# Silu and the last steps of the group statistics move from VectorE to Pool

## What is computed

```
x = x + L0(gn(x))     # a lattice of 4 x 4 convolution cells with relu
x = x + L1(gn(x))     # a convolution with circular padding
x = x + L2(gn(x))     # spline convolution: silu(p) * base + sum of 8 cubic splines(p) * weights, + bias
x = x + L3(gn(x))     # a plain 3 x 3 convolution, + bias
gn(v) = (v - mean) / sqrt(var + 1e-5)
```

## Time and profile before

| | |
|---|---|
| median of 3 runs | 1281.83 us (1278.43 to 1287.19) |
| the profiled execution | 1273.52 us, of which 1271.7 span |
| busy share of the span | PE 93%, PEld 70%, DVE 60%, ACT 53%, POOL 29% |
| chain that ended last | PE 62%, SPq 15%, DVE 10%, issue 5%, DMA 4%, ACT 3% |
| granted TensorE clock, mean | 0.976 |

### The profile page before, as it was taken

The page is one execution under the profiler, slowest core; times in us unless marked ns, Lnnn a source line. Parts: engine busy times, 40 slices in busy tenths (PEclk is TensorE's granted clock), DMA queues, the critical chain, the costliest instruction groups (busy, mean ns, idle before and its releaser), DMA issues.

```text
span 1271.7 us, 15020 instructions
## 1 busy us (share of the span) xinstructions
PE 1188.8 (93%) x5174; PEld 884.7 (70%) x5174; DVE 768.2 (60%) x975; ACT 674.6 (53%) x736; POOL 370.6 (29%) x544
## 2 busy tenths in 40 slices
PE   2799999999999999989999999999999987999995
PEld 2666677666666677766666677777777766777773
DVE  6799952475575522256565552236665689999962
ACT  1578853454444434354544443444445598789821
POOL 6212333434501022312222314534144331103212
PEclk9899999999999999999999999999999888999997
DMA  6899998999999768899999988879898214676774
GB/s 149 237 253 277 281 271 237 199 177 202 200 195 233 207 178 219 198 196 215 207 181 192 223 202 217 248 203 229 194 202 167 44 30 71 107 113 107 123 122 62
DMA packets 104687, 234.22 MB, mean 184 GB/s; under 512 B 36884, under 2 KB 49764, under 8 KB 96164
## 3 DMA queue, kind: packets, MB, share of 16 engines
q1 hardware_dynamic: 82624, 181.90, 65.5%
q0 software_dynamic: 15808, 24.31, 10.3%
q10 hardware_dynamic: 6180, 27.06, 6.8%
HBM read 124.15 MB, written 85.75 MB: 165 GB/s over the span
## 4 chain that ended last, share of the span: by engine, by line
PE 62%; SPq 15%; DVE 10%; issue 5%; DMA 4%; ACT 3%; POOL 0%; DVEq 0%; ACTq 0%; POOLq 0%
PE PB L1731 53%; SPq L807 12%; PE PB L1700 7%; DVE S L1560 2%; DVE S L1566 2%; DMA F<-F 1%; SPq L786 1%; DMA lattice<-S 1%; DVE S L1573 1%; DVE F L1553 1%; PE PB L1691 1%; SPq L838 1%; ACT F L1142 1%; DVE F L1453 1%; DMA S<-lattice 1%
## 5 line engine op out<-in xcount | busy, mean ns | idle before, releaser
L1731 PE MATMUL PB<-F,WA 128*96 128x512 f32 (+1 forms) x3792 | 916.8, 403 | 23.3 <-DVE F L1465 11.1
L1731 PEld LDWEIGHTS PB<-F,WA 128*96 128x96 f32 (+1 forms) x3792 | 662.7, 176 | 268.5 <-issue 19.8
L1153 ACT ACTIVATE S<-PB,BIAS 96x512 f32<-96x512 f32 (+1 forms) x320 | 212.2, 683 | 304.0 <-PE PB L1731 299.6
L1142 ACT ACTIVATE F<-S 128x2116 fp32r<-128x2116 f32 (+4 forms) x160 | 261.4, 1634 | 188.5 <-DMA lattice<-S 67.3
L1453 DVE TENSOR_TENSOR F<-S,F 128x1089 fp32r<-128x1089 f32 (+2 forms) x80 | 121.4, 1518 | 175.1 <-ACT F L1142 174.1
L1455 DVE TENSOR_TENSOR F<-S,F 128x1058 fp32r<-128x1058 f32 x64 | 80.8, 1263 | 185.5 <-ACT F L1142 185.0
L1465 DVE CAST F<-F 64x528 fp32r<-64x528 f32 (+4 forms) x304 | 183.7, 654 | 3.5
L1700 PE MATMUL PB<-F,WA 128*128 128x512 f32 x576 | 147.4, 414 | 15.1 <-DVE F L1553 15.1
L905 POOL DMA_DIRECT2D WA<-taps x76 | 54.1, 714 | 359.4 <-ACT S L1153 317.5
L1700 PEld LDWEIGHTS PB<-F,WA 128*128 128x128 f32 x576 | 112.5, 197 | 44.3 <-issue 15.8
L1456 DVE TENSOR_TENSOR F<-S,F 64x1058 fp32r<-64x1058 f32 x64 | 79.8, 1247 | 0.0
(11 more groups left out here) (130 smaller groups left out, 745.5 us busy)
## 6 DMA issues: line engine op xcount, KB each, us to landing
S<-lattice SPq DMA_DIRECT2D x448, 66.1 KB, 5.2
lattice<-S SPq DMA_DIRECT2D x32, 817.5 KB, 6.7
S<-lattice SPq DMA_DIRECT2D x160, 136.1 KB, 3.4
S<-lattice SPq DMA_DIRECT2D x72, 272.5 KB, 5.1
lattice<-S SPq DMA_DIRECT2D x52, 272.5 KB, 4.0
lattice<-S ACTq DMA_DIRECT2D x48, 272.5 KB, 4.6
lattice<-S ACTq DMA_DIRECT2D x16, 817.5 KB, 6.6
S<-lattice SPq DMA_DIRECT2D x160, 70.1 KB, 3.4
```

The source lines that it names most:

```text
L1142: act.activation(piece_view(s, h, 0), raw_view(s, h), ACT.Copy).then_inc(hi_ready, 1)
L1153: act.activation(wide(to[:, at:at + TS])[:, :, 0:RX], pixels(RING_BANK[n % SLOTS_O][0:cell.rows, :]), ACT.Relu, bias=BIAS[0:cell.rows, k:k ...
L1731: last = nc.tensor.matmul(bank, WA[0:rows, first:first + cell.rows], wide(FZ[0:rows, i % SLOTS_F, base:base + TS])[:, :, 0:RX], start=j == ...
```

## The change

Four things change. Pool computes silu instead of VectorE, in two instructions instead of one (SILU x NS, then + NS), with a semaphore between them, and silu's low part. The tail on VectorE keeps only the copy out of PSUM; the square, a negation of the second column and the difference go to Pool, into its norm, which waits for its own steps. The squares of the statistics get a tile of their own (MSQ), since NV is now Pool's. In Pool's order silu(0) and silu_low(0) stand right after the clearing of NS3, silu(1) and silu_low(1) between norm(1,5) and norm(1,7), and for each later image silu(b), silu_low(b), norm(2, b - 2) and from b = 5 on the output transfers of image b - 5 follow one another. The copies of x come five steps behind their loads instead of two.

```diff
-    X_SPLITS = {(k, b + 2): image for (k, b), image in X_LOADS.items()}
+    X_SPLITS = {divmod(k * B + b + 5, B): image for (k, b), image in X_LOADS.items()}
...
             def norm(par, images, n):
 
                 pool.wait_ge(nv_ready, n)
+                pool.tensor_tensor(NV[:, par], GM[:, par, 0], GM[:, par, 0], ALU.mult).then_inc(pool_norm, 1)
+                pool.tensor_scalar(GM[:, par, 1], GM[:, par, 1], -1.0, None, ALU.mult).then_inc(pool_norm, 1)
+                pool.wait_ge(pool_norm, 4 * n - 2)
+                pool.tensor_tensor(VE[:, par], GM[:, par, 1], NV[:, par], ALU.subtract).then_inc(pool_norm, 1)
+                pool.wait_ge(pool_norm, 4 * n - 1)
                 pool.tensor_tensor(RS[:, images], VE[:, par], NHALF[:, par], ALU.pow).then_inc(pool_norm, 1)
-                pool.wait_ge(pool_norm, n)
+                pool.wait_ge(pool_norm, 4 * n)
                 pool.tensor_tensor(NBI[:, images], GM[:, par, 0], RS[:, images], ALU.mult).then_inc(norm_ready, 1)
...
+            def silu(b):
+
+                pool.wait_ge(tanh_ready, b + 1)
+                pool.tensor_tensor(SILU, SILU, NS[b % 2], ALU.mult).then_inc(silu_step, 1)
+                pool.wait_ge(silu_step, b + 1)
+                pool.tensor_tensor(SILU, SILU, NS[b % 2], ALU.add).then_inc(silu_ready, 1)
+
+            def silu_low(b):
+
+                pool.wait_ge(silu_hi, b + 1)
+                pool.tensor_tensor(FR[:, 2, 0, 1], SILU, FR[:, 2, 0, 0].bitcast(F32), ALU.subtract).then_inc(silu_lo, 1)
...
             pool.memset(NS3, 0.0).then_inc(edge_done, 1)
-            norm_event(1, 5)
-            norm_event(1, 6)
-            norm_event(1, 7)
+            silu(0)
+            silu_low(0)
...
-            for b in range(B - 2):
-                norm_event(2, b)
-                if 1 <= b < B - 3:
-                    out_part(b - 1, out_dmas(b - 1))
+            norm_event(1, 5)
+            silu(1)
+            norm_event(1, 6)
+            silu_low(1)
+            norm_event(1, 7)
+            for b in range(2, B):
+                silu(b)
+                silu_low(b)
+                norm_event(2, b - 2)
+                if b >= 5:
+                    out_part(b - 5, out_dmas(b - 5))
+            out_part(B - 5, out_dmas(B - 5))
             norm_event(2, B - 2)
...
                 nc.vector.tensor_scalar(g, STAT_BANK[n % 2][:, 2 * cols.start:2 * cols.stop], scale, None, ALU.mult)\
-                    .then_inc(dve_step, 1)
-                dve.wait_ge(dve_step, next(steps))
-                m, v = GM[:, cols, 0], GM[:, cols, 1]
-                nc.vector.tensor_tensor(NV[:, cols], m, m, ALU.mult).then_inc(dve_step, 1)
-                dve.wait_ge(dve_step, next(steps))
-                nc.vector.scalar_tensor_tensor(VE[:, cols], NV[:, cols], -1.0, v, ALU.mult, ALU.subtract)\
                     .then_inc(nv_ready, 1)
...
-            def silu(b):
-
-                dve.wait_ge(tanh_ready, b + 1)
-                nc.vector.scalar_tensor_tensor(SILU, SILU, 1.0, NS[b % 2], ALU.add, ALU.mult).then_inc(silu_ready, 1)
-
-            def silu_low(b):
-
-                dve.wait_ge(silu_hi, b + 1)
-                nc.vector.tensor_tensor(FR[:, 2, 0, 1], SILU, FR[:, 2, 0, 0].bitcast(F32), ALU.subtract)\
-                    .then_inc(silu_lo, 1)
...
-            silu(0)
...
-                if g == 0:
-                    silu(b)
-                else:
-                    silu_low(b)
```

More of the change, by code:

```diff
@@ L268, in build @@
         NV = sb("NV", [P, B])
+        MSQ = sb("MSQ", [P, B])
         VE = sb("VE", [P, B])
@@ L403, in build @@
         tanh_ready, silu_ready = sem("tanh_ready"), sem("silu_ready")
+        silu_step = sem("silu_step")
         silu_hi, silu_lo = sem("silu_hi"), sem("silu_lo")
@@ L1329, in squares @@
                 m, v = MV[:, cols, 0], MV[:, cols, 1]
-                nc.vector.tensor_tensor(NV[:, cols], m, m, ALU.mult).then_inc(dve_step, 1)
+                nc.vector.tensor_tensor(MSQ[:, cols], m, m, ALU.mult).then_inc(dve_step, 1)
                 dve.wait_ge(dve_step, next(steps))
-                nc.vector.scalar_tensor_tensor(v, v, GN_EPS, NV[:, cols], ALU.add, ALU.add).then_inc(mv_ready, 1)
+                nc.vector.scalar_tensor_tensor(v, v, GN_EPS, MSQ[:, cols], ALU.add, ALU.add).then_inc(mv_ready, 1)
             def group_stats(cols, n, scale=-1.0):
```

## The result

The changed kernel takes 1313.88 us in the median (1310.88 to 1315.19, 4 runs), the kernel before in the same session 1281.15 (1278.43 to 1287.19, 4 runs). The ratio is 1.0235 with a 95% interval of 1.0207 to 1.0263: slower by 2.3%. The profiled execution took 1314.65 us, 1312.8 of them span.

What follows compares the result with a forecast made beforehand. VectorE was taken to bound three image periods, a halo-copy loop the earlier ones. Start 8.3, image 1 2, holds 8.4 and end 0.3 sum to +19 us, on the median 1281.8 giving 1301; range 1284 to 1313.

Steps and rivals of the forecast that it cites:

- The start, +8.3: Start of the spline stage: silu(0), late in Pool's queue, delays TensorE's start; +8.3 us taken, at least +3.5, worked through +9.3.
- the trace's queue: Start: Pool's queue as the trace before has it plus three more small steps, silu(0) done at 1051.2, +7.0 us.
- Image 1, +2: Image 1: norm(1,5) ahead of silu(1) on Pool repeats the start's delay; 0 to +8 us, +2 taken.
- Several steps fall beside an update: Image 1: reason for taking +2 us: several steps run beside an update and its statistics, which don't hold Pool.
- takes the next delay: Image 1 into image 2: ScalarE's idle 6.21 us at image 2 was to absorb the next delay.
- The holds, +8.4: Images 2 to 7: Pool's silu holds VectorE 1.2 us each; 3.6 for images 2 to 4, 4.8 for 5 to 7.
- The end, +0.3: Kernel end: the last norm's three more steps, 0.19 us and a semaphore each, less two VectorE steps; +0.3 us.
- At zero: Copies of x three steps later, and Pool's output issues moved by one image: zero cost each, the latter with thin cover.
- That Pool doesn't hold VectorE: First rival, spline stage: Pool waits for VectorE but doesn't hold it; +6.7 us, 1288; chance 0.22.
- that it is free: Second rival, not slower: Pool runs freely beside VectorE at its unloaded price; +0.9 us, 1283; chance 0.08.
- The third: Third rival: norm, output transfers and silu queue on Pool from image 5, silu(6), silu(7) late; +31 us, 1312; chance 0.15.

Runs made afterwards that it cites:

- both_first: Changed kernel with silu(0) ahead of norm(1,4) and the edge casts, and silu(1) ahead of norm(1,5), in Pool's queue: 1298.03 us, ratio 1.0109.
- silu1_first: Changed kernel with silu(1) ahead of the five steps of norm(1,5) in Pool's queue: 1309.15 us, ratio 1.0197.
- x_back: Changed kernel with the copies of x two steps behind their loads again: 1313.23 us, ratio 1.0223 to the kernel before.

## Why the prediction was right, and where its size was off

The direction and the mechanisms held: slower, by Pool's place in the queue and by the holds. The size did not: +19 forecast, +32.7 measured, just outside the top of the range. By its own steps:

**The start, +8.3, measured +9.2.** silu_hi(0) waits for Pool, and TensorE idles 8.88 us at B. The schedule worked through step by step had Pool done at 1053.5, 18.0 us behind A; it was 1064.20, 17.6 behind A. It gave +9.3, and taking a value below it, towards "the trace's queue", only made it worse. both_first shows the cause: with silu(0) moved ahead, the start is 23.1.

**Image 1, +2, measured +8.9. This is the step that failed.** It had two arguments. "Several steps fall beside an update" was wrong: the tail that releases norm(1,5) stands behind that update in VectorE's queue, so the steps meet basis, inner, outer and feature_lo in a row, 9.1 us. That ScalarE's idle 6.21 at image 2 "takes the next delay" was wrong because it named the wrong cover. In the trace of the kernel after, ScalarE's wait for the halo copies is indeed gone: feature_hi at 1111.70 has no idle time before it. Yet TensorE starts late: feature_lo of image 2, at 1119.98, stands in VectorE's queue behind inner and outer at 1113.18 and 1116.60, and these behind the inner at 1101.04, which waited 9.47 us for squares that ScalarE could only make after silu_hi(1). VectorE's idle time there was 0.66 us, and that was the whole cover. silu1_first bore it out: 7.1 of the 8.9 us return when the five steps stand behind silu(1). In the kernel after, the rest goes with holds in the same chain, on the square of the mean (1.08 instead of 0.16), inner (3.50) and outer (3.45), which the relief of VectorE makes up in part.

**The holds, +8.4, measured +9.6 in the five periods.** Of the 8.4, 1.2 was for feature_lo of image 2, which stands ahead of C and took 2.41, not held (the holds there fell on inner and outer), so 7.2 is what answers to the 9.6. The price was about right: Pool's 528 columns take 1.29 to 1.33 us (1.2 taken), a hold 1.10 to 1.15 (1.2). The three full periods cost 4.9 against 4.8, but part of that is luck: they cost 0.6, 1.7 and 2.5, not 1.6 each, because how many of Pool's reads meet a two-input instruction varies, and 1.0 of the last is VectorE waiting for a TensorE at a lower clock. The two loop-bound ones among the five cost 2.5 and 2.2 instead of 1.2 each. Of the first, 1.3 is idle time ahead of image 3, 4.30 instead of 3.01, as forecast; the other 1.2 is that the 42 matmuls ahead of it take 12.95 us instead of 11.73, behind an idle time of 6.81 instead of 2.63. So TensorE's idle time cost a second time through the granted clock, 0.87 in that window against 0.93; from 1120.0 to 1128.0 it is 0.50, the lower of the two levels (1.2 GHz of 2.4). No term had that. In the second period it is the same: 12.91 instead of 11.74 behind an idle time of 4.30 instead of 3.01, and 0.90 of idle time ahead of image 4 where before there was none.

**The end, +0.3, measured +2.4.** 1.5 of it is again the clock: the 42 matmuls of image 7 take 11.74 us instead of 10.22, after 2.08 us of idle time instead of 1.05, at a granted clock of 0.85 instead of 1.00 (1254.20 to 1265.78, and 1215.46 to 1225.51 before). The rest is about the size of two norms in a row, where I counted one; no run tests that.

**At zero:** the copies of x (x_back shows it) and Pool's output transfers. last_update, which would have waited for those, is released by TensorE alone, as this group by line of the kernel after shows (the idle time of 8.6 us is 8.1 for TensorE).

```profile
L1561 DVE SCALAR_TENSOR_TENSOR OT<-PB,OB,X 64x512 f32<-64x512 f32 x16 | 12.0, 747 | 8.6 <-PE PB L1705 8.1 <-issue 0.3
```

**The rivals.** That Pool doesn't hold VectorE fell with the first 3.53 row, that it is free with the first 2.2 us step. The third, Pool as a bound of its own, is nearest in total, 1312, but not in its mechanism: in the full periods Pool is busy, its waits included, 12.8 to 19.1 of some 26 us, and VectorE is the one that is full. One part of it did happen: silu_hi(6) waits 2.28 us for Pool (1223.92), but VectorE has no idle time behind that until 1242.

## What to carry to other kernels

Work moved to an engine off the critical path takes its place in that engine's queue: add up what stands ahead of it there, each small step at the length of the neighbour's instruction it must wait for, and put the moved work first if someone on the path waits for it. When you call a delay covered, walk every engine's queue between the delay and the next fixed point; here the cover was the smallest idle time among them (VectorE's 0.66 us), not the largest. Between Pool and VectorE count columns read: a read by Pool that meets a VectorE instruction with two SBUF inputs was paid by VectorE nearly in full, 1.10 to 1.15 of some 1.3 us. Not every read meets one: the 11.3 us on the three lines are about ten holds, of 24 Pool instructions of 528 columns.

## What the runs showed of the hardware that I had not expected

- A waiting Pool instruction gets in between two VectorE instructions that follow one another without a gap, and the second is then held, 1.1 us for 528 columns (silu_low at 1115.22 above, with inner and outer). So in these rows neither engine starves the other; they take turns, one instruction each, and a chain on Pool of five one-column steps costs 9.1 us while VectorE loses nothing visible to them (basis, inner and outer, 1080.00 to 1086.89, stay at 2.35 to 2.36).
- The hold reaches small instructions: VectorE's one-column square of the mean, 0.16 us at rest, takes 1.08 beside Pool's product of 528 columns (1111.72 to 1113.05), as this row of VectorE in the kernel after shows.

```profile
1111.99 1.08 DVE L1356 TENSOR_TENSOR MSQ<-MV 128x1 f32<-128x1 f32 x1
```

- A Pool instruction that only writes, the clearing of 528 columns, runs beside a two-input VectorE instruction at its full 0.54 us and costs it nothing.
